# Narrower clears behind scatters, none in the last bursts, and final loads, sums and stores spread over tiles

## The reference, cut to what matters

```python
x = x + attn_a(layernorm(x))
x = x + ffn(layernorm(x))     # 8 experts, the best 2 for each token
x = x + attn_b(layernorm(x))
x = x + ffn(layernorm(x))

# ffn, for each token m and its two experts n with weights ew:
h = x @ Wl1[n] + bl1[n]                       # 128 -> 512, halves a and b
y[n] = (silu(a) * b) @ Wl2[n] + bl2[n]        # 256 -> 128
out[m] = sum over n of ew[m, n] * y[n]
```

## Time and profile before

| what | us |
| --- | --- |
| median of 3 runs | 1126.68 (1126.1 to 1127.27) |
| profiled execution, its own time | 1127.07 |
| span of its trace | 1125.2 |
| busy: PE, DVE, ACT, POOL | 813.4, 710.8, 574.7, 790.0 |
| indirect transfers to the queues (L554), 256 | 293.6 |
| indirect transfers of results (L566), 284 | 281.7 |
| clears (L542), 540 | 183.3 |
| chain that ended last, share of PE, DVE, ACT, POOL, DMA | 37%, 17%, 14%, 12%, 8% |

### The profile page before, as it was taken

One profiled execution on the slowest core, in us unless ns is written; L12 is line 12 of the kernel. 1 busy time (PEld: TensorE's weight loads), 2 busy tenths in 40 slices (PEclk: granted clock), 3 DMA queues, 4 the chain that ended last, 5 costly groups with the idle time before them and its releaser, 6 DMA issues.

```text
span 1125.2 us, 19439 instructions
## 1 busy us (share of the span) xinstructions
PE 813.4 (72%) x4480; PEld 651.4 (58%) x4481; DVE 710.8 (63%) x2600; ACT 574.7 (51%) x1588; POOL 790.0 (70%) x1123
## 2 busy tenths in 40 slices
PE   4687787876229999998755655775620899999971
PEld 2476666666219999987433323443420798888861
DVE  4588888875615555455478887778840355566655
ACT  2787677771113333335588888887620333433320
POOL 2007868776747888888611788898888388888864
PEclk9788888785559999999878778877755899999986
DMA  7022322122345555557201333311223457767784
GB/s 191 20 57 88 96 84 77 57 66 71 97 119 177 180 185 183 178 180 225 67 18 58 102 103 105 105 52 36 67 68 99 139 183 230 248 195 236 231 272 128
DMA packets 159973, 142.66 MB, mean 127 GB/s; under 512 B 17539, under 2 KB 132876, under 8 KB 159792
## 3 DMA queue, kind: packets, MB, share of 16 engines
q1 hardware_dynamic: 121744, 70.98, 22.8%
q10 hardware_dynamic: 20448, 37.23, 10.1%
q0 software_dynamic: 17728, 33.88, 8.8%
HBM read 93.47 MB, written 50.37 MB: 128 GB/s over the span
## 4 chain that ended last, share of the span: by engine, by line
PE 37%; DVE 17%; ACT 14%; POOL 12%; issue 9%; DMA 8%; SPq 1%; DVEq 1%; POOLq 0%; ACTq 0%; another core or an unknown queue 0%
PE banks L1055 11%; PE banks L1075 6%; POOL queue_dram L554 4%; POOL result_dram L566 4%; PE banks L931 4%; DMA xtile<-queue_dram 4%; POOL spacer L542 4%; PE banks L957 4%; DVE stats L1229 3%; DMA result_dram<-ytile,result_row 2%; ACT hmix L651 2%; ACT qkv L749 2%; PE banks L1110 2%; PE banks L1111 2%; PE banks L945 2%
## 5 line engine op out<-in xcount | busy, mean ns | idle before, releaser
L554 POOL DMA_INDIRECT queue_dram<-hffn,place_i x256 | 293.6, 1147 | 159.5 <-remote 115.4
L566 POOL DMA_INDIRECT result_dram<-ytile,result_row x284 | 281.7, 992 | 97.4 <-issue 42.2
L1055 PE MATMUL banks<-xt,tile_up 128*128 128x256 f32 x1136 | 275.3, 386 | 8.7 <-DVE gated L1407 8.7
L765 ACT ACTIVATE gated<-banks,tile_bias 128x256 f32<-128x256 f32 x284 | 119.3, 471 | 246.8 <-PE banks L1055 218.0
L1055 PEld LDWEIGHTS banks<-xt,tile_up 128*128 128x128 f32 x1136 | 208.7, 194 | 33.6 <-issue 7.2
L1407 DVE SCALAR_TENSOR_TENSOR gated<-banks,tile_bias,gated 128x256 f32<-128x256 f32 x284 | 124.2, 479 | 131.6 <-ACT gated L765 126.2
L542 POOL MEMSET spacer<- 128x256 f32 x540 | 183.3, 339 | 0.2
L1075 PE MATMUL banks<-wdown_sb,gated 128*128 x1136 | 151.9, 277 | 1.8 <-DVE ytile L1415 1.8
L1075 PEld LDWEIGHTS banks<-wdown_sb,gated 128*128 128x128 f32 x1136 | 139.8, 194 | 2.6 <-issue 2.4
L1063 PE MATMUL banks<-k_sb,xtile 128*128 128x128 f32 x284 | 56.4, 281 | 75.8 <-DMA xtile<-queue_dram 75.8
L931 PE MATMUL banks<-k_sb,hmix 128*128 128x128 f32 x128 | 29.9, 380 | 100.2 <-ACT hmix L651 71.0
(11 more groups left out here) (213 smaller groups left out, 1576.6 us busy)
## 6 DMA issues: line engine op xcount, KB each, us to landing
tile_up<-w_up ACTq DMA_DIRECT2D x142, 256.0 KB
xtile<-queue_dram SPq DMA_DIRECT2D x142, 130.0 KB
qkv<-result_dram SPq DMA_DIRECT2D x28, 512.0 KB, 5.6
x_dram<-xres SPq DMA_DIRECT2D x32, 256.0 KB, 3.2
result_dram<-ytile,result_row POOLq DMA_INDIRECT x284
xin<-x SPq DMA_DIRECT2D x16, 256.0 KB, 4.5
xold<-x SPq DMA_DIRECT2D x16, 256.0 KB, 3.2
queue_dram<-hffn,place_i POOLq DMA_INDIRECT x256, 2.4
```

The costliest lines, as they stand in the source:

```text
L554: nc.gpsimd.indirect_dma_start(queue_dram, bass.IndirectOffsetOnAxis(ap=place_i[s][:, at:at + 1], axis=0), hffn[s][c][:, j, :], None).then ...
L566: nc.gpsimd.indirect_dma_start(result_dram, bass.IndirectOffsetOnAxis(ap=result_row[i % SLOTS][:, h:h + 1], axis=0), ytile[i % SLOTS][:, h ...
L765: last = nc.scalar.activation(gated[i % GSLOTS][:, h, :], ps_up[i % 2][:, h, :], ACT.Silu, bias=tile_bias[i % STEP][:, h:h + 1])
L1055: last = nc.tensor.matmul(ps_up[i % 2][:, h, :], tile_up[i % WSLOTS][:, h * P:(h + 1) * P], xt[i % 2][:], start=True, stop=True)
```

## The change

The clears are 176 columns wide in place of 256 everywhere. In bursts 8 and 16, the last before each expert stage, there are none. The final work has a new timetable by tile: for batches 1 to 6, tile 8m + 14 + 0 to 3 is followed by one load each on SP (x and results of chunk 0, x and results of chunk 1), tile 8m + 18 + 0 to 3 by one half sum each on DVE, and, for batches 1 to 5, tiles 8m + 24 and 8m + 25 by one store each (tile 65 has no tile load left to follow, so the last store of batch 5 comes behind them). Batches 7 and 8 stay behind the last tile. Slots alternate by batch. DVE's groups are written out, no longer a loop.

```diff
@@ -41,7 +41,7 @@
-SPACERS, SPACER_W = 8, 256
+SPACERS, SPACER_W = 8, 176
...
-        FIRST_USES, SECOND_USES, FINAL_FIRST = 6, 2, 1
+        FINAL_FIRST = 1
+        LOAD_AT, SUM_AT, STORE_AT = 14, 18, 24
+
+        def final_slot(m, c):
+
+            return (m + 1) % 2 * HALVES + c
...
                 else:
-                    for i in range(STEP):
-                        reload(0, i)
-                    for n in range(1, LAST):
-                        for i in range(STEP):
-                            reload(n, i)
-                            if i == STEP // 2:
-                                landed(n, needed(1) - STEP)
-                                load_final(n, 0)
-                        store_final(n, 0, n)
-                    load_final(LAST, 0)
-                    for i in range(FINAL - SLOTS):
-                        reload(LAST, i)
-                        if i == 2:
-                            landed(0, needed(6))
-                            load_final(6, 2)
-                    store_final(5, 0, 5)
+                    for t in range(TILES_RUN - SLOTS):
+                        n, i = divmod(t, STEP)
+                        reload(n, i)
+                        m, at = divmod(t - LOAD_AT, NE)
+                        if 1 <= m <= 6 and at < 2 * HALVES:
+                            if at == 0:
+                                landed(0, needed(m))
+                            load_final(m, at // HALVES, at % HALVES)
+                        m, at = divmod(t - STORE_AT, NE)
+                        if 1 <= m <= 5 and at < HALVES:
+                            store_final(m, at)
+                    load_final(6, 1, 1)
+                    store_final(5, 1)
                     landed(0, needed(7))
-                    load_final(7, 0)
-                    store_final(6, 2, 6)
-                    load_final_x(8, 2)
+                    for c in range(HALVES):
+                        load_final(7, c, 0)
+                        load_final(7, c, 1)
+                    for c in range(HALVES):
+                        store_final(6, c)
+                        load_final(8, c, 0)
                     landed(0, TILES_RUN)
-                    load_final_y(8, 2)
-                    store_final(7, 0, 7)
-                    store_final(8, 2, 8)
-
-            def load_final_x(m, i):
-                for c in range(HALVES):
-                    sp.dma_start(final_x[i + c], rows(x3_dram, m * HALVES + (c - HALVES))).then_inc(final_in[i + c], 16)
-
-            def load_final_y(m, i):
-                for c in range(HALVES):
-                    load_results(m * HALVES + (c - HALVES), final_y[i + c], final_in[i + c])
-
-            def load_final(m, i):
-                load_final_x(m, i)
-                load_final_y(m, i)
-
-            def store_final(m, i, count):
-                for c in range(HALVES):
-                    sp.wait_ge(final_ready, FINAL_FIRST + count * HALVES + (c + 1 - HALVES))
-                    sp.dma_start(rows(out, m * HALVES + (c - HALVES)), final_out[i + c][:]).then_inc(out_stored[i + c], 16)
+                    for c in range(HALVES):
+                        load_final(8, c, 1)
+                    for m in (7, 8):
+                        for c in range(HALVES):
+                            store_final(m, c)
+
+            def load_final(m, c, results):
+
+                slot, chunk = final_slot(m, c), m * HALVES + (c - HALVES)
+                if results:
+                    load_results(chunk, final_y[slot], final_in[slot])
+                else:
+                    sp.dma_start(final_x[slot], rows(x3_dram, chunk)).then_inc(final_in[slot], 16)
+
+            def store_final(m, c):
+
+                slot, chunk = final_slot(m, c), m * HALVES + (c - HALVES)
+                sp.wait_ge(final_ready, FINAL_FIRST + chunk + 1)
+                sp.dma_start(rows(out, chunk), final_out[slot][:]).then_inc(out_stored[slot], 16)
 
...
-            def scatter(m, s):
+            def scatter(m, s, spread=True):
...
-                            space(at, BT * TOPK)
+                            if spread:
+                                space(at, BT * TOPK)
...
-            scatter(8, 0)
+            scatter(8, 0, spread=False)
...
-                scatter(b + BATCH, b % 2)
+                scatter(b + BATCH, b % 2, spread=b < BATCH)
...
-            def final_sums(m, c, i, use):
-
-                if c == 0:
+            def final_sum(m, c, k):
+
+                if c == 0 and k == 0:
                     dve.wait_ge(final_ready, m * HALVES + (FINAL_FIRST - HALVES))
                     settle(nc.vector.tensor_copy(gate[:].rearrange("p (j k) -> p j k", k=TOPK), gate_all[:, bass.ds(m * BT - BT, BT), :]))
+                i, use = final_slot(m, c), (m + 1) // 2
                 y = final_y[i].rearrange("p (j k) d -> p j k d", k=TOPK)
-                dve.wait_ge(out_stored[i], use * 16)
-                dve.wait_ge(final_in[i], use * 32)
-                for k in range(TOPK):
-                    for j in range(TPC):
-                        col = (c * TPC + j) * TOPK + k
-                        last = nc.vector.scalar_tensor_tensor(final_out[i][:, j, :], y[:, j, k, :], gate[:, col:col + 1],
-                                                              (final_out if k else final_x)[i][:, j, :], ALU.mult, ALU.add)
-                    if k == 0:
-                        settle(last)
-                last.then_inc(final_ready, 1)
+                if k == 0:
+                    dve.wait_ge(out_stored[i], use * 16)
+                    dve.wait_ge(final_in[i], use * 32)
+                else:
+                    dve.wait_ge(final_first, m * HALVES + (c + 1 - HALVES))
+                for j in range(TPC):
+                    col = (c * TPC + j) * TOPK + k
+                    last = nc.vector.scalar_tensor_tensor(final_out[i][:, j, :], y[:, j, k, :], gate[:, col:col + 1],
+                                                          (final_out if k else final_x)[i][:, j, :], ALU.mult, ALU.add)
+                last.then_inc(final_ready if k else final_first, 1)
 
             def experts(f):
                 def place_rows(n, i):
...
-                        elif left == FINAL:
-                            if i in (2, 3):
-                                final_sums(5, i - 2, i - 2, 5)
-                            if i in (5, 6):
-                                final_sums(6, i - 5, HALVES + i - 5, 1)
-                        elif batch is not None and i + HALVES >= STEP:
-                            final_sums(batch, i + HALVES - STEP, i + HALVES - STEP, batch)
+                        elif f == SECOND:
+                            m, at = divmod(n * STEP + i - SUM_AT, NE)
+                            if 1 <= m <= 6 and at < HALVES * TOPK:
+                                final_sum(m, at // TOPK, at % TOPK)
 
...
-                    steps(0, 2 * STEP)
-                    with dve.Fori(1, LAST) as n:
-                        begin()
-                        steps(n, 2 * STEP, n)
+                    for n in range(LAST):
+                        steps(n, 2 * STEP)
                 steps(LAST, FINAL)
                 if f == SECOND:
-                    for c in both:
-                        final_sums(7, c, c, 6)
-                    for c in both:
-                        final_sums(8, c, HALVES + c, 2)
+                    for m in (7, 8):
+                        for c in both:
+                            for k in range(TOPK):
+                                final_sum(m, c, k)
 
```

More of the change, by code:

```diff
@@ L318, in program @@
         final_in, out_stored = ([sem(f"{name}{i}") for i in range(RING)] for name in ("final_in", "out_stored"))
-        final_ready = sem("final_ready")
+        final_first, final_ready = sem("final_first"), sem("final_ready")
         block = ctx.enter_context(nc.Block())
@@ L529, in _ @@
             experts(SECOND)
-            for i in range(HALVES):
-                sp.wait_ge(out_stored[i], 16 * (FIRST_USES + 1))
-                sp.wait_ge(out_stored[HALVES + i], 16 * (SECOND_USES + 1))
+            for i in range(RING):
+                sp.wait_ge(out_stored[i], 16 * (BATCH // 2 + 1))
         @block.gpsimd
@@ L1416, in add_bias, with steps @@
                                             down_bias_sb[:, bass.ds(e * D, D)][:, None, :].to_broadcast([P, XPARTS, D]), ALU.add).then_inc(ytile_ready, 1)
-                def steps(n, left, batch=None):
+                def steps(n, left):
                     e = read(mybir.EngineType.DVE, tile_expert[0:1, bass.ds(n * STEP, min(STEP + 4, left))], NE - 1)
```

## The result

The changed kernel takes a median of 1094.2 us (1093.75 to 1095.79, 4 runs) against 1126.39 (1123.36 to 1127.27, 4 runs): 0.9725 of the time before, 95% interval 0.9698 to 0.9752. The profiled execution took 1094.39, its span is 1092.5, so it is 32.7 shorter than the profiled execution before.

What follows compares the result with a forecast made beforehand. Bounds: POOL's 2.95 us a tile against PE's 2.84, and final loads and sums in the second stage. Gains 6.2 + 6.0 + 8.3 + 18.7 + 0.5 = 39.7 off 1127.07 gave 1087.4, forecast 1087 (1081 to 1093).

Steps and rivals of the forecast that it cites:

- Clears of 176: Each clear behind a POOL scatter: 80 fewer columns save 0.072 us, bringing POOL to 2.80 a tile.
- No clears in the last bursts: Bursts 8 and 16 before the expert stages: each of fifteen removed clears saves 0.41 us, 6.2 a burst.
- First stage: First expert stage: POOL's period falls under PE's, so no lag builds up and 6.0 of 6.3 us returns.
- Bursts elsewhere: Attention and mixing stages: narrower clears only end in longer waits for POOL, so zero, with ±2 us.
- Second stage: Second expert stage: spreading final loads, stores and sums removes PE's waits, giving back 18.7 us of 20.2 lost.
- The backlog model: Second expert stage: spread loads and stores leave tile loads landing after 5.7 us at most, under the 7.6 PE bears.
- Tail: End of the second expert stage: seven shorter POOL periods bring 0.5 us; what follows the last scatter is unchanged.
- (a): Rival: back-to-back scatters lengthen by what the clears took, so the two bursts give nothing: 1099.4 us; chance 0.10.
- (c): Rival: a clear costs the same at 176 columns, so POOL stays at 2.95 a tile: 1100 us; chance 0.05.
- (d): Rival: each of 24 half sums in the second expert stage holds a scatter for 1.14: 1109 us; chance 0.03.
- (b): Rival: the second stage's load backlog is larger than reckoned, so half its gain stays away: 1096 us; chance 0.12.
- (e): Rival: closer scatters are held in all expert stages, making the kernel slower, 1155 us in one case; chance 0.03.

## Why the prediction was right, and where not

**The time.** The forecast was 1087, with 1081 to 1093 at a chance of 0.60. The measured 1094.2 lies 1.2 above that, inside the 1081 to 1100 that was given 0.82. The places where the gain was looked for were the right ones, and its largest part came as worked out; one step was mis-sized and one left something out.

**The bound.** That POOL's 2.95 a tile stood behind the first stage's losses, and the final loads and sums behind the second's, held up. Spread, the loads and sums let PE run 157.69 of 158.00, and with POOL quicker the first stage lost 2.5 over 190.3 where it had lost 6.3.

**Clears of 176.** Said 0.072 each; 0.066 was measured. The term was right for what a clear costs POOL. That this was all a clear could do rested on the quick kind of chip, the only kind that the rows before came from.

**No clears in the last bursts.** Said 6.2 a burst, from 0.41 a clear; measured 15 x 0.195 = 2.9 of spacing. This is the term that was mis-sized. It was taken as a middle between 0.33 and 0.49, with the gap of 0.17 either staying or going. The gap did neither; it grew to 0.30. The row it leaned on, four plain transfers without a gap, was of another kind of transfer. In burst 8 only 2.14 came, since two of its scatters took 1.13 and 1.80 where they had been 0.96 and 1.28 and a pause behind the first is 1.97 for 1.76; another 1.1 was there before its first scatter (299.94 and 298.82), and 0.5 behind its last. The 1.1 lies within the spread between executions: in three other traces with the changed kernel's code up to there burst 8 starts at 296.86, 298.14 and 301.33. From the first scatter of burst 14 to the last of 16, the 77.1 of the three bursts became 70.4: 2.9 from the gap, 2.1 from narrower clears as said, and some 1.6 from a pause of 1.73 in POOL that the trace before has at 849.96 and the one after has not.

**First stage.** Said 6.0, measured 3.7. The step "no lag builds up" left out POOL's pauses: 0.3 to 0.9 over the usual gap at tiles 12, 24, 36 and 48, and one of 1.9 at tile 56, which the trace before has too (at 511.37). With 0.04 a tile in hand POOL doesn't make them up, and one of them met two loads of 512 KB. Taking the loads apart gives 2.1 back, and a POOL with more in hand (clears of 32) 1.9, both against the changed kernel on their chip.

**Bursts elsewhere.** Said zero, with ±2: the 1.1 up to burst 8, and -0.35 from tile 70 of the first stage to burst 14 (793.22 - 537.13 and 786.05 - 529.61).

**Second stage.** Said 18.7, measured 19.3, and it takes both parts of the change: the spread work alone gives 13.6 on a quick chip, and POOL's narrower clears the rest (196.92 to 191.92 between the two kernels on the last chip). Other traces of the changed kernel's second stage have 191.92, 192.26 and 192.51, so 19.3 is the best of four, and 18.0 the least. The 1.5 left for tiles 36 and 60 were not needed there; the 1.0 lost in the result stand at tiles 52 and 69. The backlog model held in that there is no wait for xtile in the stage. Its size did not: the tile loads issued between 980 and 1020 land after 5.1 in the median and after 6.8 at most (L425), where 5.7 was said for the slowest. So 0.8 of cover is left under the 7.6, where 1.9 was reckoned.

**Tail.** Said 0.5, measured -0.7. The forecast put the last scatter near 1072 and it came at 1079.02; 6.4 of that was missing before the second stage began (14.1 gained there for 20.5 said). POOL ended as far behind PE as before, for the same reason as in the first stage: 2.81 a tile and pauses against 2.84.

So 32.7 came of the 39.7 of the sum: 2.4 short up to the first stage (3.8 for 6.2), 2.3 in the first stage, 1.7 in the mixing stage and its bursts, 1.2 at the end, 0.6 over in the second. Of the rivals, (a) had the right place (the two bursts) and too large a price, (c) and (d) fell, and (b), at 1096, gave nearly the measured time by a mechanism that isn't there: the second stage, from which it took 9.4, is the one that came in full. (e), closer scatters do harm, is false on the quick chips: 32 columns are better still on the one where they were measured. On the slow chips its direction is right with another victim: not the scatters but the engines beside them.

## What to carry to other kernels

A spacer between two issues hides part of a gap that is there anyway: price its removal by the distance from issue to issue with and without it, not by its own length. An engine that is quicker than its consumer by 1% has not stopped being the bound, as long as its pauses are larger than what it gains back between them. And time a change of spacing on more than one chip: here closer scatters gave over 1% on a quick chip (32 columns for 176) and cost 2% on either of the two slow chips (176 for 256).

## What was not expected of the hardware

- Two indirect scatters of POOL stand 1.26 apart, 0.96 and a gap of 0.30; with a clear between, the gap behind the clear is 0.17.
- POOL paused 2.03 between the two scatters of tile 56 in both expert stages of the changed kernel, with nothing in the trace to wait for, by 2.0 in every other kernel on a quick chip, and by 1.9 to 2.0 in every kernel with clears on a slow chip (256 or 176 columns), so it doesn't belong to a kind of chip. Its cause was not looked for.
- On two of four chips the same program took 4% longer (1173 and 1175 for 1126 and 1129). Scatters and the granted clock were as elsewhere, and ACT stood idle behind matmuls whose records were over, the more the closer the scatters stood (no clears: 63.9 in nine waits at one place). In the expert stages the stalls come at a regular beat: in the kernel without clears every sixth result scatter starts late, at 480.39, 490.42, 500.56, 510.59, 520.61 and so on in POOL's timeline. The traces of these chips lack releasers for many waits ("remote", "issue"). The Trainium skill says (NOTIFIC — Programmer's Manual, When the ring fills and Overflow) that a full queue of records by default drops the new ones, with no sign but a flag on the next record that lands. That would fit the missing releasers; no run here shows it, nor whether the signal to ACT, the matmul or something else was late. That stays open.
